# Mixing weights of four expert layers: from a TensorE spread to transfers out of one partition

## What is computed

```python
probs = softmax(x @ gate_w + gate_b)              # 8 experts, 16 in layer 2
cw = top-2 of probs, zero elsewhere                # renormalised in layers 1 and 2
out = sum_e cw[:, e] * (gelu(x @ W1[e] + b1[e]) @ W2[e] + b2[e])        # layers 0, 1, 3
out = sum_e cw[:, e] * ((silu(x @ w1[e]) * (x @ w2[e])) @ w3[e])         # layer 2
```

## Time and profile before

| | us |
|---|---|
| median of 3 runs (1145.42 to 1151.36) | 1147.89 |
| the profiled execution, its own time | 1151.5 |
| its span | 1149.7 |
| TensorE busy | 925.7 (81%) |
| VectorE busy | 655.4 (57%) |
| ScalarE busy | 447.8 (39%) |
| GpSimd busy | 230.8 (20%) |
| expert layers 0 to 3, in the span | 115.0, 94.0, 240.4, 115.2 |

### The profile page before, as it was taken

One profiled execution on the slowest core, in us unless ns is written; L12 is line 12 of the kernel. 1 busy time (PEld: TensorE's weight loads), 2 busy tenths in 40 slices (PEclk: granted clock), 3 DMA queues, 4 the chain that ended last, 5 costly groups with the idle time before them and its releaser, 6 DMA issues.

```text
span 1149.7 us, 18333 instructions
## 1 busy us (share of the span) xinstructions
PE 925.7 (81%) x6235; PEld 447.6 (39%) x6235; DVE 655.4 (57%) x2102; ACT 447.8 (39%) x785; POOL 230.8 (20%) x393
## 2 busy tenths in 40 slices
PE   4876747996899999856868984999999967757996
PEld 1222212222567676642216762333333334532222
DVE  6787855653345554435556554757576655345653
ACT  2211225653444444324433222434343324645653
POOL 0344552101323332132210003101000011021200
PEclk9777968997589999976786555999999975767998
DMA  9300000000000000000000000000000000000001
GB/s 176 57 20 8 9 7 0 1 0 1 1 3 2 3 2 2 2 1 0 1 1 0 0 0 0 1 1 0 1 1 1 1 1 0 0 1 0 1 1 37
DMA packets 23225, 9.94 MB, mean 9 GB/s; under 512 B 14166, under 2 KB 22506, under 8 KB 23146
## 3 DMA queue, kind: packets, MB, share of 16 engines
q1 hardware_dynamic: 22122, 7.85, 3.7%
q0 software_dynamic: 1024, 1.05, 0.5%
HBM read 7.85 MB, written 1.05 MB: 8 GB/s over the span
## 4 chain that ended last, share of the span: by engine, by line
PE 62%; DVE 18%; issue 8%; ACT 6%; POOL 4%; DMA 1%; DVEq 0%; SPq 0%; ACTq 0%; POOLq 0%
PE ps L642 15%; PE ps L666 8%; PE ps L1061 4%; PE ps L330 3%; DVE best L461 2%; DVE code L465 2%; PE ps L1344 2%; DVE work L899 2%; PE ps L1106 2%; PE ps L1326 2%; PE ps L604 2%; PE ps L654 2%; PE ps L652 2%; PE ps L1033 2%; PE ps L1056 2%
## 5 line engine op out<-in xcount | busy, mean ns | idle before, releaser
L642 PE MATMUL ps<-xT,wall 64*128 64x512 f32 x576 | 166.6, 659 | 1.4 <-ACT work L777 1.4
L666 PE MATMUL ps<-work,down 128*64 128x512 f32 x576 | 156.0, 621 | 1.5 <-DVE work L899 1.1
L899 DVE TENSOR_TENSOR work<-work,ps 128x512 f32<-128x512 f32 x160 | 102.5, 682 | 79.0 <-PE ps L654 78.7
L782 ACT ACTIVATE work<-ps,b1t 128x512 f32<-128x512 f32 x160 | 100.5, 684 | 103.1 <-PE ps L642 103.0
L891 DVE TENSOR_TENSOR work<-work,ps 128x512 f32<-128x512 f32 x128 | 82.2, 683 | 66.3 <-PE ps L642 65.7
L777 ACT ACTIVATE work<-ps 128x512 f32<-128x512 f32 x128 | 69.8, 595 | 124.6 <-PE ps L642 107.8
L642 PEld LDWEIGHTS ps<-xT,wall 64*128 64x128 f32 x576 | 52.5, 198 | 97.1 <-issue 93.3
L642 PE MATMUL ps<-work,wall 64*128 64x512 f32 x256 | 73.2, 648 | 3.6 <-DVE work L891 3.3
L1210 DVE TENSOR_REDUCE maxr<-ps 128x4 f32<-128x640 f32 x32 | 26.4, 824 | 58.9 <-PE ps L1061 58.9
L1170 ACT ACTIVATE pt<-ps 128x864 f32<-128x864 f32 x32 | 28.5, 890 | 69.4 <-PE ps L1061 69.4
L666 PEld LDWEIGHTS ps<-work,down 128*64 128x64 f32 x576 | 34.0, 138 | 46.8 <-issue 35.4
(11 more groups left out here) (242 smaller groups left out, 1731.1 us busy)
## 6 DMA issues: line engine op xcount, KB each, us to landing
wall<-in_L_ffn_w_dram SPq DMA_DIRECT2D x4, 512.0 KB, 10.7
wall<-in_L_ffn_W_dram SPq DMA_DIRECT2D x4, 256.0 KB, 9.5
out_dram<-tokens SPq DMA_DIRECT2D x8, 128.0 KB, 1.7
tokens<-in_x_dram SPq DMA_DIRECT2D x1, 896.0 KB, 6.1
emb<-in_L_conv_emb_dram SPq DMA_DIRECT2D x2, 256.0 KB
down<-in_L_ffn_W_dram SPq DMA_DIRECT2D x2, 256.0 KB
down<-in_L_ffn_w_dram SPq DMA_DIRECT2D x1, 512.0 KB
zq<-in_L_conv_emb_dram,code POOLq DMA_INDIRECT x32, 2.5
```

Source lines behind the costliest of these rows:

```text
L642: ins = pe.matmul(m.ps[:, bank + half, :], m.wall[r, at + g * P:at + (g + 1) * P], src, start=True, stop=True)
L666: ins = pe.matmul(m.ps[half * C:half * C + C, 6, :], m.down[l][:, g, :], m.hid[:, n % 3, half, :], start=(g == 0 and not f["b2"]), stop=Tr ...
L782: act.activation(m.hid[:, n % 3, half, :], m.ps[:, 2 * (n % 2) + half, :], ACT.Gelu, bias=bias)\
L899: dve.tensor_tensor(y, y, m.ps[:, 4 + half, :], ALU.mult).then_inc(s.f_hw, 1)
```

## The change

The spread leaves TensorE. `weights` transposes `cw` as float32, so that `cwT` holds one row of 512 weights in each of 2E partitions (row e for the first half of the tokens, row E+e for the second). SyncE then issues, for each unit, transfers that read **one** such row (2 KB, one partition) and write it to 64 partitions of a slot of `cwb`; there are four slots, each with a semaphore. A unit has two such transfers (rows g and E+g), in layer 1 four (two experts, two halves): 64 + 64 + 128 + 64 = 320 transfers of 128 KB.

- Layers 0 and 3: the down matmuls no longer wait for a weight. Each unit's output goes to a bank of its own (4 or 5); VectorE computes (output + b2) times the slot in one instruction, and GpSimd adds the units up in `acc`. Before the first weights TensorE runs four ups and two downs.
- Layer 1: the hidden values are weighed as before, the first half on VectorE, the second on GpSimd, from slots; b2 is added by one float32 matmul.
- Layer 2: the input is scaled on GpSimd from a slot; the plain up matmuls and `silu` are double-buffered (banks 0, 1 and 4, 5).
- Gone are `parts`, `share`, `b2q`, `identb` and their preparation: 12 loads of b2, three loads of tables, GpSimd's table building in the first block, some copies on ScalarE and memsets on VectorE.
- `LEADS` gets the parts of the layer norm as steps of their own (scale, centre, norm), and longer leads.

```diff
 LEADS = {
-    4: dict(stats=8, tokens=5, logits=4, back=3, weights=1, router=4, add=3, exps=3, combine=2),
-    8: dict(stats=16, tokens=8, logits=7, back=6, weights=2, router=6, add=5, exps=4, combine=3),
+    4: dict(stats=12, scale=10, centre=9, norm=8, tokens=7, logits=6, router=6, exps=5, combine=4, weights=4, back=2, add=1),
+    8: dict(stats=17, scale=15, centre=14, norm=13, tokens=10, logits=9, router=8, exps=6, combine=5, weights=5, back=4, add=3),
...
+def ffn_sync(sp, nc, m, s, l):
+    def spread(rows, k):
+        return rows[k:k + 1, :].unsqueeze(1).broadcast_to([1, C, 512])
+    def share(n):
+        rows = m.cwT[:, n // G % 2, :]
+        if PRE[l]:
+            for half in range(2):
+                if n > 1:
+                    sp.wait_ge(*((s.f_hw, d0 + n - 1) if half == 0 else (s.f_pw, p0 + n - 1)))
+                slot, landed, _ = slot_use(m, s, l, n, half)
+                for i in range(2):
+                    sp.dma_start(slot[i * C:i * C + C, :], spread(rows, half * E + 2 * (n % G) + i)).then_inc(landed, 16)
+            return
+        if n >= SLOTS:
+            sp.wait_ge(*((s.f_hw, d0 + n - SLOTS + 1) if POST[l] else (s.f_pw, p0 + n - SLOTS + 1)))
+        slot, landed, _ = slot_use(m, s, l, n)
+        for half in range(2):
+            sp.dma_start(slot[half * C:half * C + C, :], spread(rows, half * E + n % G)).then_inc(landed, 16)
+    for sb in range(SUPERS):
+        sp.wait_ge(s.f_cwt, S0 + sb + 1)
+        for g in range(G):
+            share(sb * G + g)
...
     def weights(sb):
-        pe.wait_ge(s.f_cw, S0 + sb + 1)
+        pe.wait_ge(s.f_cwd, S0 + sb + 1)
...
-            ins = pe.transpose(out[:, t * P:(t + 1) * P], m.cwp[:, t, :, :].rearrange("p h k -> p (h k)"), m.identb[:])
+            ins = pe.transpose(m.ps[0:2 * E, 7, t * P:(t + 1) * P], m.cw[:, t * 2 * E:(t + 1) * 2 * E], m.ident[:])
...
-                ins = pe.matmul(m.ps[r, 4 + n % 2, :], m.share16[:, g, r], m.cwT[:, b, :], start=True, stop=True)
-            else:
-                ins = pe.matmul(m.ps[:, 4 + half, :], m.share[l][r, g, :], m.cwT[r, b, :], start=True, stop=True)
...
+    def down_apart(n):
+        pe.wait_ge(s.f_hid, g0 + 2 * n + 2)
+        if n > 1:
+            pe.wait_ge(s.f_hw, d0 + n - 1)
+        down(n, 4 + n % 2, True)
...
-    def weigh(n):
-        dve.wait_ge(s.f_cwb, u0 + n + 1)
-        for half in range(2):
-            dve.wait_ge(s.f_hid, g0 + 2 * n + half + 1)
-            y = m.hid[:, n % 3, half, :]
-            dve.tensor_tensor(y, y, m.ps[:, 4 + half, :], ALU.mult).then_inc(s.f_hw, 1)
+    def weigh_outputs(n):
+        slot, landed, count = slot_use(m, s, l, n)
+        dve.wait_ge(landed, count)
+        dve.wait_ge(s.f_yps, u0 + n + 1)
...
+        dve.scalar_tensor_tensor(y, m.ps[:, 4 + n % 2, :], b2, slot, ALU.add, ALU.mult).then_inc(s.f_hw, 1)
...
+    def scale_inputs(n):
+        slot, landed, count = slot_use(m, s, l, n)
+        pool.wait_ge(landed, count)
...
+        pool.tensor_tensor(m.xs[:, n % 2, :], m.xT[:, n // G % 2, :], slot, ALU.mult).then_inc(s.f_pw, 1)
+    def weigh_inner(n):
+        slot, landed, count = slot_use(m, s, l, n, 1)
+        pool.wait_ge(landed, count)
+        pool.wait_ge(s.f_hid, g0 + 2 * n + 2)
+        y = m.hid[:, n % 3, 1, :]
+        pool.tensor_tensor(y, y, slot, ALU.mult).then_inc(s.f_pw, 1)
+    def sum_outputs(n):
...
+        acc = m.acc[:, sb % 2, :]
+        pool.tensor_tensor(acc, acc, m.part[:, k % 2, :], ALU.add).then_inc(s.f_pw, 1)
```

More of the change, by code:

```diff
@@ L566, with before @@
 UNITS = [SUPERS * g for g in GROUPS]
-UNITS_BEFORE = [sum(UNITS[:l]) for l in range(len(FFN))]
-GELU_BEFORE = [sum(n for n, f in zip(UNITS[:l], FFN) if not f["gated"]) for l in range(len(FFN))]
-B2_AT = (0, 1, None, 2)
 TQ = ST // 2
-SLOT = 64
+SLOTS = 4
+PRE = [f["H"] < P for f in FFN]
+POST = [not f["gated"] and f["H"] == P for f in FFN]
+def before(counts):
+    return [sum(counts[:l]) for l in range(len(counts))]
+UNITS_BEFORE = before(UNITS)
+GELU_BEFORE = before([0 if f["gated"] else 2 * u for f, u in zip(FFN, UNITS)])
@@ L634, in extras, with up @@
             elif T > 1:
[L635 to L637 removed]
+                if f["gated"]:
+                    back(T - 2, 7, (s.f_lg, S0 + T + 1))
+                else:
+                    back(T - 2, 6)
+    def up(n, at, bank, sem, x):
         g = n % G
@@ L703, in ffn_pe @@
+    first(1)
+    if POST[l]:
+        for i in range(2):
+            first(i + 2)
+            down_apart(i)
+        weights(0)
+        for i in range(2, U):
+            first(i + 2)
+            extras(i, 2)
+            down_apart(i)
+    elif PRE[l]:
+        weights(0)
+        for i in range(U):
+            first(i + 2)
+            extras(i, 0)
+            down_weighed(i)
+    else:
+        weights(0)
         second(0)
-        first(1)
-        share(2)
         for i in range(U):
@@ L783, in unit, with extras @@
                     .then_inc(s.f_hid, 1)
-    tokens(0)
-    unit(0)
-    if not f["gated"]:
-        unit(1)
-    exps(0)
-    weights(0)
-    if f["gated"]:
-        unit(1)
-    for i in range(U):
-        unit(i + 2)
-        for T, step in due(G, i, "tokens", "exps", "weights"):
+    def extras(i, first_i):
+        for T, step in due(G, i, first_i, "tokens", "exps", "weights"):
             if step == "tokens":
@@ L801, in ffn_act @@
                 weights(T)
-        if (i + 1) % G == 0:
+    tokens(0)
+    unit(0)
+    if not f["gated"]:
+        unit(1)
+    exps(0)
+    if POST[l]:
+        unit(2)
+    weights(0)
+    if f["gated"]:
+        unit(1)
+    first_i = 0
+    if POST[l]:
+        unit(3)
+        first_i = 2
+    for i in range(first_i, U):
+        unit(i + 2)
+        extras(i, first_i)
+        if not POST[l] and (i + 1) % G == 0:
             outputs(i // G)
@@ L924, in ffn_dve @@
                     add(T - 2)
+    stats(0)
+    stats(1)
+    router(0)
+    combine(0)
+    if f["gated"]:
+        gate(0)
+    for i in range(U):
+        if POST[l]:
+            extras(i)
+            weigh_outputs(i)
+        else:
+            if f["gated"]:
+                gate(i + 1)
+            else:
+                weigh_inner(i)
+            extras(i)
     add(SUPERS - 2)
@@ new lines, in ffn_pool @@
+    for sb in range(2):
+        scale(sb)
+        centre(sb)
+        norm(sb)
+    if f["gated"]:
+        scale_inputs(0)
+        scale_inputs(1)
+    for i in range(U):
+        for T, step in due(G, i, 0, "scale", "centre", "norm"):
+            if T > 1:
+                if step == "scale":
+                    scale(T)
+                elif step == "centre":
+                    centre(T)
+                else:
+                    norm(T)
+        if POST[l]:
+            sum_outputs(i)
+        elif PRE[l]:
+            weigh_inner(i)
+        else:
+            scale_inputs(i + 2)
```

384 lines of the change are left out of this document (172 added, 212 removed).

## The result

| | before | after |
|---|---|---|
| median, four runs each on one chip, us | 1146.66 (1143.65 to 1151.36) | 1508.55 (1505.8 to 1510.23) |
| expert layers 0, 1, 2, 3, us of the span | 115, 94, 237, 115 | 177, 237, 328, 177 |
| rest of the span, us | 588 | 586 |

The changed kernel is slower: the ratio is 1.316, 95% interval 1.3123 to 1.3197. The direction was as forecast, the size was not: 2014 us were predicted, inside a range that held the result, though not inside the likeliest case's own range of 1572 to 2457.

The account below looks back on a forecast made before the run. The transfers out of single partitions were taken to bound the changed kernel: 691 us for the rest, starts and ends plus 1327 of transfers is 2018, less 3.6 from profiled execution to median gives 2014 us; range 1055 to 2480.

Parts of the forecast that it names:

- the likeliest case's own range: Whole kernel if the transfers bound it (chance 0.60): 1572 us with always two at a time, 2457 all in a row.
- What bounds the kernel: Whole kernel before: TensorE busy 81% of the span; expert layers 564.6 us, the other 585.1 left nearly alone.
- A transfer out of one partition is served by one slow place: Expert layers' weight transfers: one source partition gives all sixteen engines 22 to 24 GB/s, so 128 KB take 5.5 us.
- I take the middle, 1327 us: All 320 transfers: between all in a row, 1770 us, and always two at a time, 885; 8.3 us a unit's two.
- the stated lower bound, 885: All 320 transfers of the expert layers, if always two run at a time: 885 us.
- The starts and ends: Expert layers, beside the transfers: four starts of 21 us (84) and four ends of 5.
- The two waits: VectorE before L960, GpSimd before its product in layer 2: idle time put down to DMA, some 5 us a unit.
- would give 1150 to 1500, which neither case covers: Whole kernel: time in us at a transfer rate between the two cases, say 60 to 120 GB/s; no chance given.
- Part one: Whole kernel with transfers in time: 34 us off layers 0 and 3, 18 layer 2, 20 layer 1, 1 first block.
- the rival 1074: Whole kernel: the transfers keep up, 1074 us, within 1055 to 1110; chance 0.32.
- its 20 us rested on the leads alone: Layer 1: 71 us against 94, 20 of these 23 taken, from asking for weights four units ahead instead of one.
- The rival of hindrance: Expert layers: transfers keep up but VectorE and GpSimd hinder each other; 35 us gained, not 73, 1113 us; chance 0.08.

Follow-up runs that it names:

- the order mended: Changed kernel with copies of the rows, layer 1's transfers in turns, `weights` one unit behind `combine`: 1149.74 us; then shorter leads in layers 0 and 3 too: 1146.84 us.
- the run with many rows: Changed kernel with each 128 KB transfer reading 64 partitions of `cwT` instead of one (weights wrong, `cw` laid out wider): 1150.32 us.
- the last run: Row copies, mended order, one 256 KB transfer a unit (two in layer 1), plus shorter leads in layer 1: 1119.98 us, ratio 0.9754 to the kernel before.
- before the leads were shortened: Row copies and mended order, with one 256 KB transfer into 128 partitions a unit (two in layer 1), layer 1's leads not yet shortened: 1122.93 us.

## Why the prediction was wrong, point by point

- **What bounds the kernel** held: the rest of the span is 586 us (585 were assumed), and the four layers carry all of the difference.
- **A transfer out of one partition is served by one slow place** held. Rows 8 and 9 gave 22 to 24 GB/s for it; it is 28.5 (half of 57) to 30. This was the small part of the error: 320 transfers in a row would be 1770 us at 23.7 and 1398 at 30.
- **"I take the middle, 1327 us"** is the step that failed. It rested on the picture that the engines take their packets in the order of issue and run in step through one transfer and then the next, so that only the ends overlap. The trace shows 57 GB/s for rows eight or sixteen apart and 30 for one row or two neighbours: the overlap of two distant rows is nearly complete, and 256 KB take 4.6 us, not 8.3. By itself that makes 589 us for layers 0, 2 and 3. In layer 1, where neighbours stand behind each other, transfers overlap less (41 GB/s), 205 us. Together 794 instead of 1327. Even the stated lower bound, 885, was too high, since one place is faster than the packets' 23.7. What was missing in the text is that an order of issue decides which rows meet: layers 0, 2 and 3 alternate between places, layer 1 doesn't, and one sum for all four hid that. How two transfers in one queue come to overlap so fully, no run shows. The prediction foresaw 290 us for layer 1 and it is 237, and 560 for layer 2 and it is 328.
- **The starts and ends**, 104 us, are 126 by what is left over. That the first transfers are waited for too would lengthen them; it was not measured apart.
- **The two waits** are the ones named, at VectorE's L960 and GpSimd's product in layer 2, at 4.1 us a unit in layer 0 where some 5 were said. The sentence that 60 to 120 GB/s "would give 1150 to 1500, which neither case covers" was closer than the forecast. Such a case should have had a chance of its own.
- **Part one (1078, the rival 1074)** would have been wrong as well. With fast transfers the same order of work takes 1150. Layers 0 and 3 gain nothing instead of 17 us each, as TensorE waits behind `combine` and behind the first weighing; with the order mended they gain 14 to 16, so the sum was nearly right on what the engines' work is worth and wrong that it comes by itself. (Some 0.5 us of each wait behind `combine` belong to the wider sums of these runs, which the changed kernel lacks.) Layer 2 gains 2 to 3 us instead of 18: a gated unit became 2.93 us against 3.11, 0.18 a unit and not 0.24, and other waits ate the rest. Layer 1 gains nothing, 96.8 us at best against 93.9, which the prediction had named as the way in which it could be wrong apart from the transfers: its 20 us rested on the leads alone.
- **The rival of hindrance** (VectorE and GpSimd taking turns) is visible. VectorE in order of time in layer 0 of the kernel after; the operation has two inputs in SBUF and took 0.17 us in the kernel before (the median of 16):

```profile
274.93 0.96 DVE L899 TENSOR_TENSOR prob<-ex,prob 128x8 f32<-128x8 f32 x1
```

GpSimd's addition begins 0.31 us earlier and lasts 1.26; VectorE's product ends with it (274.62 + 1.26 = 275.88 against 275.89). The Trainium skill states such a lock ("SBUF — State Buffer", section "Who interferes with whom"), and this row agrees. It costs 0.8 us, and is not the only one: in the run with many rows such products stretched by 1.3 us stand ahead of a wait of TensorE of 4.08 us, and in layer 1 of the last run VectorE is busy 8.5 us longer. No run separates what this takes from the whole. VectorE's L960, with one input in PSUM, shows none of it: 751 ns on average over 64, in layers where GpSimd is busy with additions in most units.
- **Open.** Why layer 1 gains nothing isn't settled. In the last run the transfer engines are used to 0.36 there and GpSimd still waits 40.3 us for slots (27.0 before the leads were shortened). ScalarE writes `cwT` at 522.1 and at 544.2 us, and GpSimd's first product of it starts at 528.0 and 549.3, 5 to 6 us later, after waits of 8.2 and 4.9. So it looks like the way through `cwT` and transfer, not the rate; no run took that way apart. The hindrance on VectorE is the other candidate there, since TensorE waits 8.8 us of this layer for `combine` (5.9 before the leads were shortened).

## What to carry to other kernels

Before a transfer replaces an engine's work, count the source's partitions as well as the destination's: a broadcast out of one partition ran at 30 GB/s with the transfer engines busy to 0.89, and every unit waited for it. The same bytes out of eight to sixteen partitions, in one wide transfer, cost little: in layer 0 of the last run VectorE waits 5.2 us for slots in all, in layer 2 GpSimd 16.0. Layer 1 still waits more. Where a transfer has two sources, cost the overlap by the order in which they are issued and give each end of it a chance of its own. And a sum of work removed is only collected if the steps that remain don't stand right behind what they wait for: one number in the order table was worth 13 us in each of two layers.

## What the runs showed of the hardware that was not expected

- 28 to 30 GB/s is what one neighbourhood of source partitions gives to all transfer engines together. Two places add up to 57, and the transfer engines show a share near 0.9 all the while.
- Two transfers with neighbouring source rows behind each other in the queue gave 41 GB/s, and 53 when they took turns with distant ones.
- SyncE issued 50 of these transfers in 41 us, 0.82 us each (rows 11 show 0.60 for a load; what waits for free slots are in it is not known). Four narrow transfers a unit in place of two gained nothing: 243.7 us against 240.7 for layer 2, with 238.4 and 240.7 for the same code of that layer in two other runs.
- VectorE's sums of two SBUF operands, 128x128, took 0.28 us each as the median and up to 1.35 beside GpSimd's instructions on 128x512 operands (L920 in the last run).
